# A transformer layer on eight cores: the normalisation's apply goes from GpSimd to VectorE, the router weights' evacuation to ScalarE

## What is computed

```python
x = x + layernorm(attn(layernorm(x)))            # 8 x 4096 x 1024
x = x + layernorm(ffn(layernorm(x)))

def attn(x):     # windows of 128 tokens after a roll by -64; 16 heads of 64
    qkv = xw @ w_qkv + b_qkv                     # masked: only within each half of 64
    attn = softmax(where(mask == 0, -9e15, q @ k.T / 8))
    return roll(attn @ v @ w_o + b_o, 64)

def ffn(x):      # 16 experts, top 2, inner size 512, and a shared expert
    r = sigmoid(x @ gate_w + gate_b)
    v, i = top_k(r, 2); v = v / sum(v)
    mlp = lambda wg, wu, wd: (silu(x @ wg) * (x @ wu)) @ wd
    return x + mlp(shared) + sum_k v_k * mlp(expert i_k)
```

## Time and profile before

| | |
|---|---|
| two runs | 5033.47 and 5597.49 us (median 5315.48) |
| profiled execution | 5041.47 us |
| its span, slowest core (fastest) | 5039.9 us (5023.3 us) |
| PE, PEld busy | 3721.1 us (74%), 2020.4 us (40%) |
| DVE, ACT, POOL busy | 1603.6 us (32%), 821.3 us (16%), 125.4 us (2%) |

### The profile page before, as it was taken

One profiled execution on the slowest core, in us unless ns is written; L12 is line 12 of the kernel. 1 busy time (PEld: TensorE's weight loads), 2 busy tenths in 40 slices (PEclk: granted clock), 3 DMA queues, 4 the chain that ended last, 5 costly groups with the idle time before them and its releaser, 6 DMA issues.

```text
span 5039.9 us, 68827 instructions; the slowest of 8 cores (5023.3 to 5039.9 us)
## 1 busy us (share of the span) xinstructions
PE 3721.1 (74%) x22032; PEld 2020.4 (40%) x22032; DVE 1603.6 (32%) x3804; ACT 821.3 (16%) x1981; POOL 125.4 (2%) x128
## 2 busy tenths in 40 slices
PE   0465445599679859958975985995798599589688
PEld 0232222255335425524542542553354255245355
DVE  0420112422342352243234234224423522432333
ACT  0210000211211221121112112112112211211111
POOL 0000000000000000000000000000000000000000
PEclk9787777699779969978986996997899699789889
DMA  9067777045225405513531650461254055135345
GB/s 183 2 130 157 170 167 176 28 163 209 80 82 214 156 18 186 189 61 120 212 120 42 213 186 11 167 213 72 92 213 147 17 198 190 48 131 207 110 161 224
DMA packets 137917, 688.78 MB, mean 137 GB/s; under 512 B 11744, under 2 KB 46560, under 8 KB 65776
## 3 DMA queue, kind: packets, MB, share of 16 engines
q1 hardware_dynamic: 89792, 621.96, 34.3%
q0 software_dynamic: 47792, 62.43, 8.3%
HBM read 676.51 MB, written 70.25 MB: 148 GB/s over the span
## 4 chain that ended last, share of the span: by engine, by line
PE 62%; DVE 11%; DMA 10%; DVEq 6%; issue 5%; ACT 4%; another core or an unknown queue 2%; ACTq 0%; POOL 0%; SPq 0%; POOLq 0%
PE PSA L769 18%; PE PSA L786 17%; PE PSA L828 16%; DVEq L89 5%; PE PSA L444 5%; DMA wu_sb<-ewu 4%; DMA wd_sb<-ewd 3%; DVE psb L537 2%; PE PSA L474 2%; ACT psb L522 2%; DMA scrd<-wd_sb 1%; PE PSA L646 1%; DMA scru<-wu_sb 1%; DVE ssum L529 1%
## 5 line engine op out<-in xcount | busy, mean ns | idle before, releaser
L769 PE MATMUL PSA<-z_fm,wg_sb 128*128 128x384 f16 (+1 forms) x5984 | 1054.2, 337 | 231.3 <-DMA wu_sb<-ewu 200.0
L797 DVE TENSOR_TENSOR us<-PSA,slabA 128x384 f16<-128x384 f32 (+1 forms) x704 | 384.3, 546 | 2180.7 <-PE PSA L786 2180.6
L828 PE MATMUL PSA<-wd_sb,hs 128*128 128x512 f16 x4352 | 996.7, 387 | 63.0 <-DMA wd_sb<-ewd 63.0
L786 PE MATMUL PSA<-z_fm,wu_sb 128*128 128x384 f16 (+1 forms) x5984 | 979.0, 321 | 9.9 <-DVE us L794 8.9
L769 PEld LDWEIGHTS PSA<-z_fm,wg_sb 128*128 128x128 f16 x5984 | 602.7, 102 | 673.4 <-issue 330.9
L786 PEld LDWEIGHTS PSA<-z_fm,wu_sb 128*128 128x128 f16 x5984 | 578.5, 98 | 382.0 <-issue 28.2
L774 ACT ACTIVATE gs<-PSA 128x384 f16<-128x384 f32 (+1 forms) x748 | 355.9, 480 | 2183.4 <-PE PSA L769 2182.9
L828 PEld LDWEIGHTS PSA<-wd_sb,hs 128*128 128x128 f16 x4352 | 431.8, 99 | 581.0 <-issue 106.6
L410 PE MATMUL PSA<-ids,z_tm 128*128 128x128 f16 x512 | 63.7, 288 | 531.5 <-DVE z_fm L418 230.7
L550 PE MATMUL PSA<-ids,psb 128*128 128x128 f16 x256 | 41.5, 297 | 349.8 <-DVE psb L537 349.8
L807 DVE TENSOR_TENSOR hs<-gs,us 128x384 f16<-128x384 f16 (+1 forms) x748 | 263.6, 352 | 62.4 <-issue 4.3
(11 more groups left out here) (89 smaller groups left out, 1609.3 us busy)
## 6 DMA issues: line engine op xcount, KB each, us to landing
wg_sb<-scrg SPq DMA_DIRECT2D x170, 1024.0 KB, 6.2
wu_sb<-scru SPq DMA_DIRECT2D x170, 1024.0 KB, 8.6
wd_sb<-scrd SPq DMA_DIRECT2D x170, 1024.0 KB, 7.1
scrg<-wg_sb SPq DMA_DIRECT2D x17, 1024.0 KB, 4.1
scru<-wu_sb SPq DMA_DIRECT2D x17, 1024.0 KB, 6.4
scrd<-wd_sb SPq DMA_DIRECT2D x17, 1024.0 KB, 4.7
wg_sb<-ewg POOLq DMA_DIRECT2D x16, 1024.0 KB, 11.7
wu_sb<-ewu POOLq DMA_DIRECT2D x16, 1024.0 KB, 16.1
```

The source lines that it names most:

```text
L769: last = e.matmul(PS[:, b, 0:ST], wg_sb[:, wb_i, kc, 128 * i:128 * i + 128], z1_fm[:, kc, 0:ST], start=(kc == 0), stop=(kc == 7))
L786: last = e.matmul(PS[:, b, 0:ST], wu_sb[:, wb_i, kc, 128 * i:128 * i + 128], z1_fm[:, kc, 0:ST], start=(kc == 0), stop=(kc == 7))
L797: em = k.emit("dve", lambda e, i=i, b=b, hp_=eidx % 2, eidx=eidx, ST=ST: e.tensor_tensor(out=us[:, hp_, i, 0:ST], in0=PS[:, b, 0:ST], in1= ...
L828: last = e.matmul(PS[:, bb, :], hs[:, hp_, i, 128 * tq:128 * tq + 128], wd_sb[:, wb_i, i, 512 * jh:512 * jh + 512], start=(first and i == ...
```

## The change

Three instructions of the code go to another engine. The apply of the head (`emit_head_q`) and that of the middle normalisation (`ln_stats_apply`) go from GpSimd to VectorE, in their place in the order of the text. The evacuation of the router weights goes to ScalarE for all 16 experts, where VectorE did the even ones. Operands, shapes, types and all else stay.

```diff
@@ emit_head_q, L351
-        am = k.emit("gp", lambda e, q=q: e.tensor_scalar(
+        am = k.emit("dve", lambda e, q=q: e.tensor_scalar(
             out=z1_tm[:, q, :], in0=xa[:, q, :],
             scalar1=rstds[:, 0, q:q + 1], scalar2=nmr[:, 0, q:q + 1],
             op0=ALU.mult, op1=ALU.add),
@@ ln_stats_apply, L388
-                am = k.emit("gp", lambda e, q=q, stage=stage: e.tensor_scalar(
+                am = k.emit("dve", lambda e, q=q, stage=stage: e.tensor_scalar(
                     out=dst_view[:, q, :], in0=src_view[:, q, :],
                     scalar1=rstds[:, stage, q:q + 1], scalar2=nmr[:, stage, q:q + 1],
                     op0=ALU.mult, op1=ALU.add),
@@ the router weights, L869 to L875
-                    if ei2 % 2 == 0:
-                        em = k.emit("dve", lambda e, ei2=ei2, b=b, ST=ST: e.tensor_copy(
-                            wbc[:, ei2, 0:ST], PS[:, b, 0:ST]), waits=later(pm), inc=True)
-                    else:
-                        em = k.emit("act", lambda e, ei2=ei2, b=b, ST=ST: e.activation(
-                            out=wbc[:, ei2, 0:ST], in_=PS[:, b, 0:ST], func=AF.Identity,
-                            bias=0.0, scale=1.0), waits=later(pm), inc=True)
+                    em = k.emit("act", lambda e, ei2=ei2, b=b, ST=ST: e.activation(
+                        out=wbc[:, ei2, 0:ST], in_=PS[:, b, 0:ST], func=AF.Identity,
+                        bias=0.0, scale=1.0), waits=later(pm), inc=True)
```

## The result

| | before | after |
|---|---|---|
| median of all runs | 5086.47 us (16 runs, 5033.47 to 5606.58) | 5134.55 us (17 runs, 5057.1 to 5521.64) |
| ratio after / before | | 1.0066, 95% interval 1.0039 to 1.0094 |
| profiled execution | 5041.47 us (span 5039.9) | 5065.27 us (span 5063.7) |
| DVE, ACT, POOL busy | 1603.6, 821.3, 125.4 us | 1607.7, 857.8, 48.8 us |

The changed kernel is 0.66% slower. The interval of the ratio lies above 1, and the difference is within the 2% that count as no change. In about half of its executions the cores of one die, or parts of both, had a lower granted clock; every ratio in this document leaves such executions out, the medians do not. The forecast was 5078 us, the range 5045 to 5100. The executions that the ratio uses lie at 5057 to 5107 us with their middle at 5072.6, but the median of all runs, 5134.55, is above the range.

A forecast was written before the change was run, and what follows sets the result against it. The prediction took VectorE to set the pace in the middle normalisation, with TensorE waiting for it. Middle 28.8, head 0 and 2.7, router 5.4 made 36.9 us on 5041.5: 5078 us, range 5045 to 5100.

The forecast's parts named there:

- I forecast an execution like it: Last step of the sum: the median will be near the profiled execution's 5041.5 us plus 36.9, so 5078 us.
- The middle normalisation: Its 32 applies, moved into VectorE's order uncovered: 28.8 us more, 2.70 per pass of 384 tokens, 1.80 in the last.
- The step of 0.90 us: Delay of VectorE's next instruction by one apply, taken from L669; bounds 0.62 and 1.32 us.
- The price of f16: VectorE's apply from f32 to f16 keeps the 813 ns of the f32 to f32 row L669.
- rival B: f16 output is slow on VectorE: step 1.32 us for 35 applies, 46 us, total 5093 to 5100 us; chance 0.07.
- The head: Head's apply on VectorE: 29 hidden in the experts at cost 0, three uncovered at the kernel's start, 2.7 us.
- The router: Router weights' evacuation all on ScalarE: matmul pairs 1.35 instead of 1.28 us, 77 x 0.07 = 5.4 us more.
- A: Applies cheaper on VectorE, each of 32 saving 0.43 us, 14 in all: 5033 us; chance 0.10, together with overlooked cover.
- C: Slower by over 2%: TensorE's clock rises two groups later in each pass, 114 us more, 5193 us; chance 0.03.

## Why the prediction was right or wrong

**The forecast of the difference came close, that of the time did not.** 36.9 us is a ratio of 1.0073. The measured ones are 1.0066, whose interval holds it, and 1.0055, whose interval ends at 1.0071. The step that failed is the last of the sum, "I forecast an execution like it". It took the profiled execution for what the median would be, although one of the two runs shown was 5597 us. The median of 17 runs is 5134.55 us, because half of the executions took 5134 to 5522 us, and a range of 5045 to 5100 has no room for them. The applies and the router are not at fault for that; the range was. Part of the closeness in the difference is luck, since the stages of the profiled executions add up to 25.5 us, 11 less than forecast, of which 4.6 and 1.5 us are in the two terms below and the rest in places that the forecast left out.

**The middle normalisation: right in mechanism, 4.6 us too high.** The step of 0.90 us was 0.91 to 0.92, and the statistics start 3.67 us apart (forecast 3.66). But the three applies add 2.3 to 2.4 us a pass from L371 to the gate instead of 2.70. The wait for GpSimd's count fell away, worth 0.29 us by the run that puts it back. And the last pass adds 0.67 instead of 1.80. The sentence that failed is "and the last, of 256 tokens, has it with two blocks of 128 tokens instead of three". With two blocks the last apply was not covered: the earlier trace rows has TensorE waiting 12 times for L388 in 11 passes, and the twelfth is this one. Sum 24.2 instead of 28.8.

**The price of f16.** The apply took 812 ns, and rival B is out. The Trainium skill's rule (VectorE: DVE Perf Modes, "What auto-detection actually checks") gave the same, and this case now shows it for f32 to f16 as well.

**The head.** Nothing within the experts, as forecast: 5.59 us of VectorE's wait are left. At the start 2.7 us were forecast. The first QKV matmul came at 140.6 to 142.3 us in the six kernels where GpSimd has the head's apply, and at 142.9 to 145.3 in the seven where VectorE has it. The means are 2.9 us apart, so this term was right. Not forecast were the 3.9 us less at the ends of the passes.

**The router.** 5.4 us were forecast and 3.9 measured in the whole change, but not by the way that was forecast. The pair is 1.31 us and not 1.35, as the release took 0.25 us and not 0.28; that makes 77 x 0.03 = 2.3 us, and the router alone cost 1.9. The rest is the clock. The prediction had it at its lower level all through the router. In the kernel before it was still at the upper level over most of the first pair in 63 of 80 cases, and the longer middle normalisation took that away. That the second wait makes the release dear was right, and the run without it showed so.

**The rivals.** A (cheaper applies) holds only where GpSimd was on the path, in the last pass: 0.19 us of one apply. C is out; the experts took no longer. Yet the clock does move the QKV stage by up to 1.5 us in a pass, in both directions and with no trend that these runs could settle. For differences of half a per cent this limits how well a sum can hit.

By stages the sum is 24.2 (L371 to the gate) - 2.1 (L646 to the first L371) + 3.9 (router) + 4.9 (start) - 3.9 (ends) - 2.8 (experts) + 1.3 (the other three) = 25.5 us, and the profiled executions differ by 23.8 us. No run explains three of these: the -2.8 in the experts, the -2.1, and 2.0 of the 4.9, which lie in the first pass's QKV and attention, where the change edits nothing. The ratios of many executions stand for 28 to 33 us. The difference between the two was not resolved.

## What to carry to other kernels

Moving work to a faster engine costs its full step when that engine's order sets the pace and the slower one worked beside it. Ask what the new engine does at that moment, not which engine is faster. Count the semaphores ahead of a waiting instruction: one that is long met, behind the one that is awaited, is paid each time, and waits for two producers on one engine become one. A stretch that gets longer can also cost time in the next one, where the clock then falls sooner. Before putting a sum against a median, look at how many of the runs shown are like the one profiled.

## What was not expected of the hardware

- A semaphore wait that is already met cost TensorE 0.10 us when it stood behind the awaited one (pairs of 1.31 against 1.21 us), and nothing that shows when it stood ahead of it (0.147 against 0.144 us).
- GpSimd's apply (one input, 128x1024 f32) and VectorE's addition of two SBUF tensors of that size took 1.74 and 2.05 us when they overlapped, 1.20 and 1.23 when they did not. Beside `bn_stats` the apply took 1.20.
- The same 128 matmuls took 22.0 to 23.5 us in different passes of one kernel, at a mean granted clock of 0.94 to 0.88.
